# The decay factors of a state-space mixer's chunks: from matmul sums and exponentials to a VectorE scan over factors read back from memory

## The chip, the core and the metric

The kernel runs on one core of a Trainium2 chip, as one program of five engines: TensorE (PE in the profile, its weight loads PEld), VectorE (DVE), ScalarE (ACT), GpSimd (POOL) and SyncE (SP), which here does nothing but issue the DMAs. Each engine takes its instructions in the order in which they are written, and they meet at semaphores. The metric is the device time of one execution, in microseconds.

## The reference

A layer of four parts works on x, 64 sequences of 32 positions with 512 channels: a mixing of the channels by a condition vector, a selective state-space mixer (the attention-like part), a small grouped convolution with a context term, and a feed-forward part with a cluster test. The change is in the second part. What matters of it:

```python
proj = jnp.einsum('bld,pd->blp', hidden_states, in_proj_w)
xBC = jax.nn.silu(conv)                      # causal, 4 taps, over 6144 channels of proj
dt_p = jax.nn.softplus(dt + dt_bias)         # 64 heads
A = -jnp.exp(A_log)
dA = jnp.exp(dt_p * A)
dtx = dt_p[..., None] * x
def step(state, inp):
    dA_t, dtx_t, B_t, C_t = inp
    state = state * dA_t[..., None, None] + dtx_t[..., None] * B_t[:, :, None, :]
    y_t = jnp.einsum('bhpn,bhn->bhp', state, C_t)
    return (state, y_t)
y = ys + x * D                               # then a group norm, silu(gate) and out_proj
```

Since a sequence has only 32 positions, the kernel doesn't run the recurrence. Written out, y at position t is the sum over s up to t of (C_t . B_s) times dA_(s+1) ... dA_t times dt_s x_s. So for each head it needs a 32x32 table of decays, the product of the factors dA after s up to t.

## The kernel before, in words

**Tiling.** The 2048 rows (64 sequences x 32 positions) are 16 tiles of 128 rows, in 4 blocks of 4 tiles. The mixer runs in 32 stages: stage n handles one group of 8 heads (g, of 8) for one block (four tiles, 512 rows); `who(n)` gives half, group and block. Two consecutive stages use the same weights, so weights are loaded and split for pairs: the even stage comes first, and the next pair's input weights are split into a high and a low part during the odd stage (`split_w_hi` on ACT, `split_w_lo` on POOL), the output weights during the even one (`split_o_hi` on ACT, `split_o_lo` on DVE). All products are done as three matmuls of high and low parts.

**Slots.** A stage has ten slots m = 0 to 9. On every engine a function `stage(n)` walks through the slots, and what an engine does in a slot is written there by hand; that is what sets the order. PE's slot is `proj(n, m)`: 12 matmuls of 512 columns into one of three PSUM banks. The first six go through ACT (`evac`), three convolution taps on DVE (`taps`) and a SiLU on ACT; slots 6 to 9 are the gate. PE may start `proj` m+3 only when the bank of m is free. Between the projections PE does, for the stage before, `Y(n-1, 2)` and `Y(n-1, 3)` in slot 2 and the output products `O(n-1, i)`, 12 matmuls each, after slots 1, 3, 4 and 5; for this stage the products C.B (`G_all`, slot 2), the turning of x (`turn_x`, slots 7 and 9) and `Y(n, 0)`, `Y(n, 1)` at the end of slot 9. O(n-1, i) needs y in a high part (`y_high`, ACT) and a low one (`y_low`, POOL).

**The decays.** The logs of the factors, dt times A, are made once for each block as a [64 heads x 2, 256] tile `da`, with the softplus done on DVE as a series of 12 steps (`dt_series`, two-input operations of 256 columns, one reciprocal). PE turns step sizes and logs in slot 6 of stages 0, 1, 16 and 17 (`dt_turn`, the stages in `TURNED`). Then in each of the 32 stages: POOL multiplies the logs, as high and low part, with a mask of s up to t (`decays`, two operations of 128x1024, slot 6); PE sums them with a triangular matrix `uf` in `decay_sums`, four matmuls of 512 columns after slot 8; ACT takes the exponential (`expo`, two operations of 512 columns and an activation table load, slot 8); and DVE multiplies the decay table `Lt` with the masked C.B products (`decayed`, slot 9 for tiles 0 and 1, slot 1 of the next stage for 2 and 3). The result, in `big`, is what `Y` multiplies with the scaled x (`dtx`).

**Blocks.** Stages 0, 15 and 16 (`BLOCK_AT`) prepare the next block beside their own work: `mix_tile` in slots 2 to 5 and `dt_product`, 12 matmuls after slot 8. The softplus series of that block ran in slot 9 (two steps) and slots 4 and 5 of the next stage.

**DMA queue.** SP issues everything in one order: for a pair u, the four output weight tiles (`load_o`, the last waits for the split in slot 7 of the even stage), then ten input weight tiles for the next pair (`load_w`, three buffers, so each waits for the split of the third one before).

## Time and profile before

| | |
|---|---|
| median of 3 runs | 1578.07 us (1577.88 to 1579.59) |
| the profiled execution | 1578.78 us, of which the span is 1576.8 us |
| mean granted TensorE clock | 0.997 |
| busy share of the span | PE 98%, PEld 80%, DVE 67%, ACT 54%, POOL 50% |
| moved by DMA | 80.5 MB, 51 GB/s on average |

The span runs from the first to the last instruction, 2.0 us less than the execution's own time. The busy time of PE is the union of its matmuls; since they are pipelined, each row of a matmul is longer than the distance to the next start. Stage 0 begins at 20 us, stage 1 at 74 us, stage 10 ends at 521 us, stage 17 begins at 804 us, and the last one ends near 1475 us. Where a group of rows has an arrow after its numbers, that is the idle time of the engine just before these instructions, and what ended it.

### The profile page before, as it was taken

The page shows a single profiled execution, that of the slowest core. Times are in us where ns is not written, and L with a number is a line of the kernel's source. Part 1 is how long each engine was busy: PE and PEld are TensorE (multiplying, and loading weights), DVE is VectorE, ACT ScalarE, POOL GpSimd, SP SyncE. Part 2 cuts the span into 40 slices and gives each one's busy share as a digit, 9 for nine tenths or more (in the row PEclk, how much of TensorE's full clock was granted, in tenths as well). Part 3 has the DMA queues.
Part 4 walks back from the last instruction along what each step waited for, and adds up shares of the span by engine and source line. Part 5 has one row for each costly group of instructions (what it writes and reads, how often), then busy time and mean ns, then how long its engine had stood idle before and what let it go on. Part 6 is the DMA issues. An engine that isn't in the chain of part 4 may idle for free. (4 is left out here: it accounts for less than half of the span.)

```text
span 1576.8 us, 32373 instructions
## 1 busy us (share of the span) xinstructions
PE 1551.4 (98%) x12991; PEld 1268.9 (80%) x12991; DVE 1049.9 (67%) x1689; ACT 850.4 (54%) x1420; POOL 783.4 (50%) x747
## 2 busy tenths in 40 slices
PE   8999999999999999999999999999999999999997
PEld 6778888888888888888877888888888888888686
DVE  5877766665666756576877656667665656666566
ACT  4654556555555555555464555556555554545542
POOL 3565554546364554545354463644545463643506
PEclk9999999999999999999999999999999999999999
DMA  5110201111120201111012111102011111103212
GB/s 201 54 49 20 63 27 55 41 41 55 35 61 8 61 28 55 41 41 54 1 55 95 41 54 35 55 10 66 28 55 41 41 54 35 43 20 91 86 42 107
DMA packets 49524, 80.54 MB, mean 51 GB/s; under 512 B 4896, under 2 KB 13600, under 8 KB 49376
## 3 DMA queue, kind: packets, MB, share of 16 engines
q1 hardware_dynamic: 49376, 78.48, 15.9%
q8 instruction: 104, 1.70, 0.4%
q14 instruction: 44, 0.36, 0.1%
HBM read 70.07 MB, written 8.39 MB: 50 GB/s over the span
## 5 line engine op out<-in xcount | busy, mean ns | idle before, releaser
L434 PE MATMUL PS<-xh,wh 128*128 128x512 f32 x1280 | 519.9, 406 | 0.6 <-DVE xl L954 0.6
L434 PE MATMUL PS<-xh,wl 128*128 128x512 f32 x1280 | 500.8, 391 | 0.0
L434 PE MATMUL PS<-xl,wh 128*128 128x512 f32 x1280 | 499.1, 390 | 0.0
L1023 DVE SCALAR_TENSOR_TENSOR cb<-PS,P,cb 128x496 f32<-128x496 f32 (+2 forms) x576 | 412.6, 716 | 126.4 <-ACT cb L755 112.8
L1318 POOL TENSOR_TENSOR wl<-rw,wh 128x512 fp32r<-128x512 f32 x160 | 207.9, 1305 | 185.7 <-ACT wh L706 185.6
L1338 POOL TENSOR_TENSOR ysum<-yq 128x256 f32<-128x256 f32 x128 | 109.5, 856 | 356.2 <-ACT yq L802 356.1
L434 PEld LDWEIGHTS PS<-xh,wl 128*128 128x128 f32 x1280 | 240.5, 188 | 53.0
L434 PEld LDWEIGHTS PS<-xh,wh 128*128 128x128 f32 x1280 | 240.9, 188 | 50.3 <-issue 1.0
L434 PEld LDWEIGHTS PS<-xl,wh 128*128 128x128 f32 x1280 | 241.4, 189 | 44.6
L755 ACT ACTIVATE cb<-PS,P 128x512 f32<-128x512 f32 x192 | 148.5, 773 | 198.1 <-PE PS L434 198.1
L547 PE MATMUL PS<-oh,yh 128*128 128x512 f32 x512 | 200.1, 391 | 1.3 <-POOL yl L1347 0.8
L547 PE MATMUL PS<-oh,yl 128*128 128x512 f32 x512 | 199.9, 391 | 0.0
L547 PE MATMUL PS<-ol,yh 128*128 128x512 f32 x512 | 199.2, 389 | 0.0
L802 ACT ACTIVATE yq<-y 128x512 f32<-128x512 f32 x128 | 81.1, 633 | 202.0 <-DVE y L1067 190.3
L1053 DVE TENSOR_TENSOR big<-Lt,gmt 128x512 f32<-128x512 f32 x128 | 102.6, 843 | 117.0 <-ACT Lt L794 117.0
L762 ACT ACTIVATE big<-PS 128x512 f32<-128x512 f32 x128 | 76.3, 596 | 147.6 <-PE PS L434 147.2
L777 ACT ACTIVATE big<-cb 128x512 f32<-128x512 f32 x192 | 119.7, 623 | 65.6 <-DVE cb L1023 65.6
L1092 DVE SCALAR_TENSOR_TENSOR acc<-PS,rs,acc 128x512 f32<-128x512 f32 x128 | 93.1, 749 | 89.1 <-issue 47.3
L1355 POOL TENSOR_TENSOR rs<-vr,mh 128x1 f32<-128x1 f32 (+1 forms) x95 | 57.1, 601 | 160.1 <-DVE vr L1082 160.1
L1043 DVE TENSOR_TENSOR dtx<-PS,dtt 128x512 f32<-128x512 f32 x128 | 82.1, 683 | 60.0 <-PE PS L477 59.7
L547 PEld LDWEIGHTS PS<-oh,yh 128*128 128x128 f32 x512 | 96.1, 188 | 21.9 <-ACT yh L809 2.2
L547 PEld LDWEIGHTS PS<-oh,yl 128*128 128x128 f32 x512 | 96.1, 188 | 20.1
(195 smaller groups left out, 2142.6 us busy)
## 6 DMA issues: line engine op xcount, KB each, us to landing
rw<-in_w_in SPq DMA_DIRECT2D x160, 256.0 KB, 2.7
ro<-in_w_out SPq DMA_DIRECT2D x64, 256.0 KB, 2.9
x2s<-acc SPq DMA_DIRECT2D x16, 256.0 KB, 3.0
out_x<-acc SPq DMA_DIRECT2D x16, 256.0 KB, 2.6
acc<-in_x SPq DMA_DIRECT2D x3, 1024.0 KB, 9.3
wh<-x2s SPq DMA_DIRECT2D x8, 256.0 KB, 3.8
wl<-x2s SPq DMA_DIRECT2D x8, 256.0 KB, 4.5
acc<-in_x SPq DMA_DIRECT2D x4, 256.0 KB, 4.6
```

What stands on the lines that cost most here:

```text
L434: mm = e.matmul(PS[:, proj_bank(n, m), :], w[:, m, 128 * k:128 * k + 128], v[:, k, a:a + 512], start=(i == 0), stop=(i == 11))
L547: mm = e.matmul(PS[:, O_bank(n, i), :], v[:, r, 128 * j:128 * j + 128], w[:, j, :], start=(q == 0), stop=(q == 11))
L755: e.activation(cb[:, z % 2, :], PS[:, proj_bank(n, m), :], ACT.Identity, bias=P[:, P_CB + c:P_CB + c + 1], scale=P[:, P_CW + 4 * c + 3:P_C ...
L762: e.activation(gate[:, m - 6, :], PS[:, proj_bank(n, m), :], ACT.Silu).then_inc(evac_ok.sem, 1)
L777: e.activation(dst, cb[:, (6 * n + m) % 2, :], ACT.Silu).then_inc(silu_ok.sem, 1)
L802: e.activation(yq[:, :], y[:, i % 2, :], ACT.Square).then_inc(yq_ok.sem, 1)
L1023: e.scalar_tensor_tensor(out=cv[:, :, d:32], in0=pv[:, :, 0:32 - d], scalar=P[:, P_CW + 4 * c + 3 - d:P_CW + 4 * c + 4 - d], in1=cv[:, :, ...
L1043: e.tensor_tensor(dtx[:, r, :].rearrange("p (j v c) -> p j v c", j=4, v=2), PS[:, b0:b0 + 2, 256 * r:256 * r + 256].rearrange("p v (j c) - ...
L1053: e.tensor_tensor(Mb[:, i % 2], bc(Lt[:, 256 * i:256 * i + 256].rearrange("p (h o t) -> p h o t", h=8, o=1), 128, 8, 2, 32), bc(gmt[:, i, ...
L1092: e.scalar_tensor_tensor(out=acc[:, T, :], in0=PS[:, O_bank(n, i), :], scalar=rs[:, i:i + 1], in1=acc[:, T, :], op0=ALU.mult, op1=ALU.add) ...
L1318: e.tensor_tensor(wl[:, m, :], rw[:, q % RW, :], f(wh[:, m, :]), ALU.subtract).then_inc(w_lo.sem, 1)
L1338: e.tensor_tensor(ysum[:, :], yq[:, 0:256], yq[:, 256:512], ALU.add).then_inc(ys1.sem, 1)
```

## The change

The 32x32 table of a head obeys a recurrence along t: L[s, t] = L[s, t-1] times dA_t, and L[s, s] = 1. The change makes the table by that recurrence, with one VectorE instruction for each stage (`tensor_tensor_scan`, multiply, then maximum): its first input `dab` holds the factors, the same row for all 32 partitions s of a sequence, with 0 for the first position of each row of 32, which resets the scan; its second, `diag`, is 1 where t = s and 0 elsewhere. The name `Lt` is kept; its columns are now ordered head, tile, position.

- The factors are made once for each block: in slot 4 of the stages in `TURNED`, ACT takes the exponential of `da` (`rates_exp`), POOL sets the first positions to 0 (`first_rates`), and SP stores them to a DRAM tensor `rates` in two DMAs of 64 partitions, in pieces of 256 bytes.
- In each stage SP reads back four pieces, each one 4 KB row of DRAM read for 32 partitions (`load_rate`, 4 x 128 KB); this waits until the scan of the stage before has read the buffer. DVE runs the scan in slot 7.
- `decay_sums`, `expo` and the POOL `decays` go, and so do two of the four turns in `dt_turn` and what split the turned logs.
- `decayed` for tiles 0 and 1 moves from slot 9 to 8.
- The series of a block has its steps in slots 1, 2 and 3 of stage 0, four each, and otherwise in slot 9 and slots 2 and 3 of the next stage. `dt_product` moves from after slot 8 to slot 7 (for blocks 1 to 3 into another PSUM bank), `dt_first` on ACT from slot 9 to 8.

The core of the diff:

```diff
+        dab = sb("dab", [128, 1024])
+        diag = sb("diag", [128, 1024])
...
+        rate_t = dt_x
...
+        def D_bank(b):
+            return PY[0] if b else PT
...
+            def store_rate(b):
+                sp.wait_ge(rate_zero, b)
+                for r in range(2):
+                    dst = bass.AP(rates.tensor, b * 32768 + 64 * r, [[128, 64], [8192, 4], [1, 64]])
+                    src = rate_t[64 * r:64 * r + 64, :].rearrange("p (q a) -> p q a", q=4)
+                    e.dma_start(dst, src).then_inc(rate_out[b].sem, 16)
+
+            def load_rate(n):
+                half, g, tb = who(n)
+                b = 2 * half + tb
+                sp.wait_ge(rate_out[b], 1)
+                if n >= 1:
+                    sp.wait_ge(L_ok, n - 1)
+                for q in range(4):
+                    src = bass.AP(rates.tensor, b * 32768 + 8192 * q + 1024 * g, [[0, 32], [1, 1024]])
+                    e.dma_start(dab[32 * q:32 * q + 32, :], src).then_inc(ld_rate.sem, 16)
+
...
                 for j in range(4):
+                    if u % 8 == 0 and j == 2:
+                        store_rate(u // 4)
+                        load_rate(2 * u)
                     load_o(u, j)
+                if u % 8:
+                    load_rate(2 * u + 1)
                 if u < 15:
                     for m in range(10):
                         load_w(u + 1, m)
+                        if u % 8 == 0 and m == 7:
+                            store_rate(u // 4 + 1)
+                        if u % 8 == 0 and m == 8:
+                            load_rate(2 * u + 1)
+                if u % 8 != 7:
+                    load_rate(2 * u + 2)
                 if u == 8:
                     for T in range(8):
...
+                if b >= 2:
+                    pe.wait_ge(acc_ok, ({2: 14, 3: 15}[b], 3))
                 i = 0
                 for k in range(4):
                     for w, v in ((wdh, xh), (wdh, xl), (wdl, xh)):
-                        mm = e.matmul(PS[0:64, PT, :], w[:, 64 * k:64 * k + 64], v[:, k, a:a + 512], start=(i == 0), stop=(i == 11))
+                        mm = e.matmul(PS[0:64, D_bank(b), :], w[:, 64 * k:64 * k + 64], v[:, k, a:a + 512], start=(i == 0), stop=(i == 11))
...
-                pe.wait_ge(d_done, b)
+                pe.wait_ge(d_step, (b, 10))
...
-                for i, src in enumerate((dr[:, 0:128], dr[:, 128:256], da[:, 0:128], da[:, 128:256])):
-                    mm = e.transpose(PS[:, SEG[0], 128 * i:128 * i + 128], src, ident)
+                for i in range(2):
+                    mm = e.transpose(PS[:, SEG[0], 128 * i:128 * i + 128], dr[:, 128 * i:128 * i + 128], ident)
                 mm.then_inc(DT_ok.sem, 1)
...
-            def decay_sums(n):
...
-                for r in range(2):
-                    if r == 0 and n - 1 in BLOCK_AT:
-                        pe.wait_ge(a_hi, BLOCK_AT[n - 1])
-                        pe.wait_ge(a_lo, BLOCK_AT[n - 1])
-                    if n >= 1:
-                        pe.wait_ge(acc_ok, (n - 1, 1 + 2 * r))
-                    else:
-                        pe.wait_ge(x_lo, 5 + 2 * r)
-                    e.matmul(PS[:, SEG[r], :], uf[:, :], avh[:, 512 * r:512 * r + 512], start=True, stop=False)
-                    e.matmul(PS[:, SEG[r], :], uf[:, :], avl[:, 512 * r:512 * r + 512], start=False, stop=True).then_inc(seg_ok.sem, 1)
...
-                    pe.wait_ge(L_ok, (n, 0))
-                    if n in BLOCK_AT:
-                        pe.wait_ge(d_max, (BLOCK_AT[n], 1))
+                    if n in TURNED:
+                        pe.wait_ge(dt_ok, TURNED[n])
...
-                    pe.wait_ge(L_ok, (n, 1))
                     pe.wait_ge(dtx_ok, (n, 1))
+                    if n in BLOCK_AT:
+                        pe.wait_ge(d_max, (BLOCK_AT[n], 1))
...
-                    if m == 8:
-                        decay_sums(n)
                         if b is not None:
                             dt_product(b)
...
                     act.wait_ge(DT_ok, b - 1)
+                    act.wait_ge(rate_out[b - 1], 1)
...
+            def rates_exp(b):
+                act.wait_ge(d_done, b)
+                e.activation(rate_t.rearrange("p (q i t) -> p q i t", q=4, i=2),
+                             da[:, :].rearrange("p (i q t) -> p q i t", i=2, q=4), ACT.Exp).then_inc(rate_exp.sem, 1)
+
             def dt_turned(b):
                 a = 4 * (b % 2)
-                dt, av = (PS[:, SEG[0], k:k + 256].rearrange("p (i r c) -> p i r c", i=2, r=2) for k in (0, 256))
                 act.wait_ge(DT_ok, b)
-                e.copy(dtt[:, a:a + 4, :].rearrange("p (r i) c -> p i r c", r=2), dt).then_inc(dt_ok.sem, 1)
-                e.copy(ah[:, a:a + 4, :].rearrange("p (r i) c -> p i r c", r=2), av).then_inc(a_hi.sem, 1)
+                e.copy(dtt[:, a:a + 4, :].rearrange("p (r i) c -> p i r c", r=2),
+                       PS[:, SEG[0], 0:256].rearrange("p (i r c) -> p i r c", i=2, r=2)).then_inc(dt_ok.sem, 1)
...
-            def expo(n):
-                for r in range(2):
-                    act.wait_ge(seg_ok, (n, r))
-                    if n >= 1:
-                        act.wait_ge(M_ok, (n - 1, 3))
-                    e.activation(Lt[:, 512 * r:512 * r + 512], PS[:, SEG[r], :], ACT.Exp).then_inc(L_ok.sem, 1)
...
-                act.wait_ge(seg_ok, (n, 1))
...
-                    if b is not None and m == 9:
+                    if b is not None and m == 8:
...
+                    if n in TURNED and m == 4:
+                        rates_exp(TURNED[n])
...
-                    if m == 8:
-                        expo(n)
...
-            def dt_turned(b):
...
+            def decays(n):
+                dve.wait_ge(ld_rate, n)
+                if n == 0:
+                    dve.wait_ge(diag_ok)
+                e.tensor_tensor_scan(Lt[:, :], dab[:, :], diag[:, :], 0.0, ALU.mult, ALU.max).then_inc(L_ok.sem, 1)
...
-                dve.wait_ge(L_ok, (n, i // 2))
+                dve.wait_ge(L_ok, n)
                 dve.wait_ge(G_masked, n)
-                e.tensor_tensor(Mb[:, i % 2], bc(Lt[:, 256 * i:256 * i + 256].rearrange("p (h o t) -> p h o t", h=8, o=1), 128, 8, 2, 32),
+                e.tensor_tensor(Mb[:, i % 2], bc(Lt[:, :].rearrange("p (h i t) -> p h i t", h=8, i=4)[:, :, i:i + 1, :], 128, 8, 2, 32),
...
-                series = {0: (0, {1: (0, 2), 2: (2, 4), 3: (4, 7), 4: (7, 9), 5: (9, 12)})}.get(n)
...
+                        e.tensor_copy(diag[:, :].rearrange("p (a t) -> p a t", a=32),
+                                      bc(C[:, C_EQ:C_EQ + 32].rearrange("p (a t) -> p a t", a=1), 128, 32, 32)).then_inc(diag_ok.sem, 1)
+                    if m == 7:
+                        decays(n)
                     if m == 8:
                         scale_turned(n, 0)
                         scale_turned(n, 1)
-                    if m == 9:
                         decayed(n, 0)
                         decayed(n, 1)
-                    if n == 0 and 1 <= m <= 5:
-                        dt_series(0, *((0, 2), (2, 4), (4, 7), (7, 9), (9, 12))[m - 1])
+                    if n == 0 and 1 <= m <= 3:
+                        dt_series(0, 4 * m - 4, 4 * m)
                     if b is not None and m == 9:
-                        dt_series(b, 0, 2)
-                    if n - 1 in BLOCK_AT and m in (4, 5):
-                        dt_series(BLOCK_AT[n - 1], *((2, 7), (7, 12))[m - 4])
-                    if m == 6 and n in TURNED:
-                        dt_turned(TURNED[n])
+                        dt_series(b, 0, 4)
+                    if n - 1 in BLOCK_AT and m in (2, 3):
+                        dt_series(BLOCK_AT[n - 1], *((4, 8), (8, 12))[m - 2])
...
-            def decays(n):
-                half, g, tb = who(n)
-                b = 2 * half + tb
-                pool.wait_ge(dt_ok, b)
-                pool.wait_ge(a_hi, b)
-                pool.wait_ge(a_lo, b)
-                if n >= 1:
-                    pool.wait_ge(O_ok, (n - 1, 3))
-                for src, dst, done in ((ah, avh, av_hi), (al, avl, av_lo)):
-                    e.tensor_tensor(dst.rearrange("p (i h t) -> p i h t", i=4, h=8),
-                                    bc(f(src[:, 4 * tb:4 * tb + 4, 8 * g:8 * g + 8]).rearrange("p i (h o) -> p i h o", o=1), 128, 4, 8, 32),
-                                    bc(C[:, C_V:C_V + 32].rearrange("p (a b t) -> p a b t", a=1, b=1), 128, 4, 8, 32),
-                                    ALU.mult).then_inc(done.sem, 1)
+            def first_rates(b):
+                pool.wait_ge(rate_exp, b)
+                e.memset(rate_t.rearrange("p (a t) -> p a t", t=32)[:, :, 0], 0.0).then_inc(rate_zero.sem, 1)
...
-                    if m == 6:
-                        decays(n)
+                    if m == 4 and n in TURNED:
+                        first_rates(TURNED[n])
...
-    cst[:, C_V:C_V + 32] = s[:, None] <= np.arange(32)[None, :]
+    cst[:, C_EQ:C_EQ + 32] = s[:, None] == np.arange(32)[None, :]
```

TensorE at the border of slots 8 and 9 of an even stage. L434 (L461 in the changed kernel) is a matmul of `proj`, with xh, xl, wh and wl the high and low parts of activations and weights; L453 and L454 are those of `decay_sums`. Before:

```order
L434 MATMUL PS<-xl,wh 128x512
L434 MATMUL PS<-xh,wl 128x512
L453 MATMUL PS<-yh,uf 128x512 [waits s_avl,s_avh]
L454 MATMUL PS<-yl,uf 128x512
L453 MATMUL PS<-yh,uf 128x512 [waits s_acc]
L454 MATMUL PS<-yl,uf 128x512
L434 MATMUL PS<-xh,wh 128x512 [waits s_ev,s_w_lo,s_w_hi]
```

With the change:

```order
L461 MATMUL PS<-xh,wh 128x512
L461 MATMUL PS<-xl,wh 128x512
L461 MATMUL PS<-xh,wl 128x512
L461 MATMUL PS<-xh,wh 128x512 [waits s_ev,s_w_lo,s_w_hi]
L461 MATMUL PS<-xl,wh 128x512
```

The four matmuls and their two waits are gone, and the projection of slot 9 follows that of slot 8.

VectorE from slot 6 to slot 9 of an even stage: acc is the accumulated output, ol the low part of the output weights, dtx the scaled and turned x, big<-Lt,gmt the product of decays and masked C.B. Before:

```order
L1092 SCALAR_TENSOR_TENSOR acc<-PS,rs,acc 128x512 [waits s_acc,s_rs,s_O]
L1011 SCALAR_TENSOR_TENSOR ol<-ro,P,oh 128x512 [waits s_o_hi] x2
L1043 TENSOR_TENSOR dtx<-PS,dtt 128x512 [waits s_T]
L1043 TENSOR_TENSOR dtx<-PS,dtt 128x512
L1011 SCALAR_TENSOR_TENSOR ol<-ro,P,oh 128x512 [waits s_o_hi]
L1053 TENSOR_TENSOR big<-Lt,gmt 128x512 [waits s_Gm,s_L]
L1053 TENSOR_TENSOR big<-Lt,gmt 128x512
L1011 SCALAR_TENSOR_TENSOR ol<-ro,P,oh 128x512 [waits s_o_hi]
```

With the change:

```order
L1096 SCALAR_TENSOR_TENSOR acc<-PS,rs,acc 128x512 [waits s_acc,s_rs,s_O]
L1015 SCALAR_TENSOR_TENSOR ol<-ro,P,oh 128x512 [waits s_o_hi]
L1010 SCALAR_TENSOR_TENSOR Lt<-dab,diag 128x1024 [waits s_ld_rate]
L1015 SCALAR_TENSOR_TENSOR ol<-ro,P,oh 128x512 [waits s_o_hi]
L1047 TENSOR_TENSOR dtx<-PS,dtt 128x512 [waits s_T]
L1047 TENSOR_TENSOR dtx<-PS,dtt 128x512
L1057 TENSOR_TENSOR big<-Lt,gmt 128x512 [waits s_Gm,s_L]
L1057 TENSOR_TENSOR big<-Lt,gmt 128x512
L1015 SCALAR_TENSOR_TENSOR ol<-ro,P,oh 128x512 [waits s_o_hi] x2
```

The scan (L1010) stands between the first two splits, behind a wait for the factors, and the decay products come ahead of the last two splits.

VectorE in slots 2 and 3 of stage 1, from the accumulation of slot 2 on; cb is a convolution tap, gmt the masked C.B, y and yg the output before and after the gate. Before:

```order
L1092 SCALAR_TENSOR_TENSOR acc<-PS,rs,acc 128x512 [waits s_rs,s_O]
L1023 SCALAR_TENSOR_TENSOR cb<-PS,P,cb 128x16x31 [waits s_ev]
L1023 SCALAR_TENSOR_TENSOR cb<-PS,P,cb 128x16x30 [waits s_tap]
L1023 SCALAR_TENSOR_TENSOR cb<-PS,P,cb 128x16x29 [waits s_tap]
L1031 TENSOR_TENSOR gmt<-PS,C 128x256 [waits s_M,s_G]
L1067 TENSOR_TENSOR y<-PS,big 128x512 [waits s_yg,s_yq,s_Y]
```

With the change:

```order
L1096 SCALAR_TENSOR_TENSOR acc<-PS,rs,acc 128x512 [waits s_rs,s_O]
L992 TENSOR_SCALAR dr<-pb 128x256 [waits s_dch]
L994 SCALAR_TENSOR_TENSOR dr<-dr,pb 128x256 [waits s_dch] x3
L1027 SCALAR_TENSOR_TENSOR cb<-PS,P,cb 128x16x31 [waits s_ev]
L1027 SCALAR_TENSOR_TENSOR cb<-PS,P,cb 128x16x30 [waits s_tap]
L1027 SCALAR_TENSOR_TENSOR cb<-PS,P,cb 128x16x29 [waits s_tap]
L1035 TENSOR_TENSOR gmt<-PS,C 128x256 [waits s_M,s_G]
L1071 TENSOR_TENSOR y<-PS,big 128x512 [waits s_yg,s_yq,s_Y]
```

Four steps of the series stand now ahead of the taps of slot 2 and of y for tile 2.

## Rows read from the trace of the kernel before

**Rows 1.** The page, busy microseconds, share of the span and instructions of each engine.
```profile
PE 1551.4 (98%) x12991; PEld 1268.9 (80%) x12991; DVE 1049.9 (67%) x1689; ACT 850.4 (54%) x1420; POOL 783.4 (50%) x747
```

**Rows 2.** Two stretches: length, busy PE, PEld, DVE, ACT, POOL, clock, DMA.
```profile
120.00:800.00 680.00, 680.00 (x5630) 557.17 (x5620) 456.26 (x698) 373.17 (x596) 342.24 (x326) 1.00 0.13 41
854.00:1400.00 546.00, 546.00 (x4606) 447.48 (x4605) 355.83 (x544) 299.65 (x475) 281.67 (x270) 1.00 0.14 43
```

**Rows 3.** PE's waits: line waited, releaser, microseconds in total, times, longest.
```profile
PE PS L453 <- issue: 4.5, 3, 2.1
PE PS L489 <- ACT big L777: 3.7, 1, 3.7
PE PS L414 <- DVE da L997: 1.0, 3, 0.4
```

**Rows 4.** PE's groups of instructions: shape, count, busy microseconds, mean ns.
```profile
L453 PE MATMUL PS<-yh,uf 128*128 128x512 f32 x64 | 25.2, 393 | 4.5 <-issue 4.5
L454 PE MATMUL PS<-yl,uf 128*128 128x512 f32 x64 | 24.9, 389 | 0.0
...
L414 PE MATMUL PS<-C,da 128*128 128x128 f32 x8 | 1.5, 273 | 0.0
```

**Rows 5.** Timeline of PE, end of stage 10: start, length, instruction.
```profile
515.88 0.39 PE L453 MATMUL PS<-yh,uf 128*128 128x512 f32 x1
...
516.78 0.39 PE L434 MATMUL PS<-xh,wh 128*128 128x512 f32 x1
...
520.24 0.46 PE L509 MATMUL PS<-big,dtx 64*64 64x64 f32 x16
```

**Rows 6.** Timeline of PE, slots 8 and 9 of stage 0.
```profile
64.58 0.40 PE L403 MATMUL PS<-xh,wdh 128*64 128x512 f32 x1
...
68.93 0.39 PE L434 MATMUL PS<-xh,wh 128*128 128x512 f32 x1
```

**Rows 7.** A stretch of stage 0, with the columns of rows 2.
```profile
66.00:68.00 2.00, 2.00 (x6) 1.10 (x5) 0.40 (x1) 0.78 (x2) 0.00 (x0) 0.50 0.15 58
```

**Rows 8.** Timeline of DVE, slots 6 to 9 of stage 10.
```profile
508.55 1.67 DVE L1011 SCALAR_TENSOR_TENSOR ol<-ro,P,oh 128x512 fp32r<-128x512 f32 x1
512.74 0.75 DVE L1011 SCALAR_TENSOR_TENSOR ol<-ro,P,oh 128x512 fp32r<-128x512 f32 x1 [2.52 <-ACT oh L713]
513.40 1.28 DVE L1043 TENSOR_TENSOR dtx<-PS,dtt 128x512 f32<-128x512 f32 x2
...
518.62 1.29 DVE L1053 TENSOR_TENSOR big<-Lt,gmt 128x512 f32<-128x512 f32 x2 [3.27 <-ACT Lt L794]
```

**Rows 9.** DVE's groups of instructions, with the columns of rows 4.
```profile
L1067 DVE TENSOR_TENSOR y<-PS,big 128x512 f32<-128x512 f32 x128 | 87.5, 684 | 31.3 <-PE PS L509 31.3
...
L981 DVE RECIPROCAL dr<-da 128x256 f32<-128x256 f32 x4 | 7.0, 1752 | 0.1
...
L993 DVE SCALAR_TENSOR_TENSOR dr<-pb,da 128x256 f32<-128x256 f32 x4 | 1.7, 423 | 0.1
```

**Rows 10.** Timeline of DVE in stage 1, the series where it stood.
```profile
97.81 1.26 DVE L987 TENSOR_SCALAR dr<-pb 128x256 f32<-128x256 f32 x1
99.11 0.88 DVE L989 SCALAR_TENSOR_TENSOR dr<-dr,pb 128x256 f32<-128x256 f32 x2
```

**Rows 11.** Timeline of POOL in stage 1: the low part of y, tile 2.
```profile
92.26 1.30 POOL L1347 TENSOR_TENSOR yl<-yg,yh 128x512 fp32r<-128x512 f32 x1
```

**Rows 12.** Timeline of PE in stage 1: the first matmul of O(0, 2).
```profile
94.64 0.39 PE L547 MATMUL PS<-oh,yh 128*128 128x512 f32 x1
```

**Rows 13.** The page, DMA issues: count, KB each, median microseconds from issue to landing.
```profile
rw<-in_w_in SPq DMA_DIRECT2D x160, 256.0 KB, 2.7
...
acc<-in_x SPq DMA_DIRECT2D x3, 1024.0 KB, 9.3
```

**Rows 14.** Timeline of SP, stage 10: the ten input weight loads.
```profile
513.94 44.93 SPq L299 DMA_DIRECT2D rw<-in_w_in  x10
```

**Rows 15.** Timeline of ACT, stage 11, slot 0: the first of these weights is split.
```profile
525.06 0.61 ACT L706 CAST wh<-rw 128x512 fp32r<-128x512 f32 x1
```

48 lines of the change are left out of this document (14 added, 34 removed).

## The prediction

> **What bounds the kernel now.** First the busy shares: TensorE is busy 98% of the span, VectorE 67%, the other two about half [rows 1]. A share near 100% could still hide a loop through another engine that ends just in time, so the next view is the busy time by stretch: from 120 to 800 us PE is busy 680.00 of 680.00 us, from 854 to 1400 us all 546, at full clock, while DVE has 456 and 356 [rows 2]. In nearly all of the 32 stages PE never waits. What it takes out of those stages comes off the time, as long as nobody else's work becomes late. Third, the list of PE's waits: 4.5 us in three places ahead of the decay sums (L453), 3.7 us once ahead of the C.B products in stage 0 (L489), 1.0 us in three places ahead of the turns (L414) [rows 3]. The first and the last of these lie on the chain softplus series, turns, split, POOL mask, decay sums, in the stages where a block's decays are first made.
>
> **What a matmul costs.** A row of the decay sums has a mean of 389 to 393 ns [rows 4], but these lengths overlap. The cost is the distance between starts: the first of the four starts at 515.88, the projection behind them at 516.78 [rows 5], so four cost 0.90 us, 0.225 each.
>
> **The sum, part by part.** It starts from the profiled execution, 1578.78 us.
>
> 1. The decay sums go from 32 stages: 32 x 0.90 = 28.8 us, all on PE's path.
> 2. Their waits go: 4.5 us, and with them the reason, since the sums' operands no longer exist. The waits ahead of the turns, 1.0 us, go as well: the series now ends in slot 3 and the turns stay in slot 6, and they wait no longer for the last step.
> 3. Eight of 16 turns go. Their busy time is 1.5 us [rows 4]; with the same overlap as above (0.225 of 0.39) that is 0.9 us.
> 4. Behind the longest of the waits, 2.1 us in stage 0, the clock fell: the granted clock is 0.50 (1.2 instead of 2.4 GHz) from 66 to 68 us [rows 7], and the 12 matmuls of `dt_product` take from 64.58 to 68.93, 4.35 us [rows 6], where 12 x 0.225 = 2.7 us would do. 1.65 us come back if PE doesn't pause there.
> Together 36.85 us.
>
> **What replaces it, and what covers it.**
>
> 5. The scan. No row shows one. From below: two-input operations take 684 ns for 512 columns and 423 ns for 256 [rows 9], 1.02 ns a column and 0.16 us fixed, so 1024 columns at that rate are 1.2 us. From above: the one row in which a column takes several passes is the reciprocal, 1752 ns for 256 columns [rows 9], 7.0 us for 1024. I take 2.3 us, twice the rate of an ordinary operation, since a multiply and a maximum that feed each other are much closer to an ordinary row than to a division. What it may take, from the timeline of an even stage [rows 8]: DVE is free after the first split at 508.55 + 1.67 = 510.22. Behind the scan are the second split 0.75, two scalings 1.28 and two decay products 1.29, together 3.32. PE wants the products for Y at 520.24 [rows 5], less the 0.90 removed: 519.34. So the scan has 519.34 - 510.22 - 3.32 = 5.8 us; at 2.3 it costs nothing. Today's products end at 518.62 + 1.29 = 519.91, 0.3 us ahead of Y: the change turns a tight chain (sums, table load, exponential, product) into one with 3.5 us to spare. Odd stages have no split there and more room. The covers are DVE's idle times of 2.52 and 3.27 us in slots 7 to 9 [rows 8]; without them 32 x 2.3 = 74 us would be at stake.
>
> The Trainium skill's page "DVE: opcode table, instruction layouts, handler registers and perf-mode slots" (section Datapath and trigger behaviour) says of the built-in scan that it "runs at half throughput". By that rule, the estimate is 2.3 us, the sum stays, and the rival of a slow scan would fall away; no run so far shows it.
>
> 6. The factor loads: 4 x 128 KB for a stage. DVE's scan waits for them, and behind it on DVE are the split, the scalings and the products, for which PE waits. They are issued when the scan before has ended, so they have a whole stage, some 44 us; even at the 9.3 us of the 1024 KB loads [rows 13] they cost DVE nothing. In the four stages where they come behind the stores of the new factors the lead is only two to three slots of some 4.5 us, against two landings in a row of 3 to 5 us each; I take nothing and leave this to the range. What is queued behind them on SP is the rival below.
>
> 7. ACT loses two exponentials and a table load a stage, POOL two operations of 1024 columns. Neither is on the path, nothing is earned.
>
> 8. The series moves earlier, and this is what costs. In stages 1 and 17 four steps now stand in slot 2, ahead of y for tile 2. A step of 256 columns beside a POOL operation took 1.26 us, later ones 0.44 each (0.88 for two) [rows 10]; so 1.26 + 3 x 0.43 = 2.55 us of delay for y. From y the way leads over ACT and POOL: the low part ends at 92.26 + 1.30 = 93.56 [rows 11], and O(0, 2) starts at 94.64 [rows 12], 1.1 us of slack. PE will wait some 1.4 us in each, 2.8 in all. Bounds: nothing if DVE catches up; with all four steps at 1.26, 5.0 - 1.1 = 3.9 each. Stage 16 has mixing tiles on PE in slots 2 and 3 and so more room; nothing is taken.
>
> 9. In stage 0 two more steps, 2 x 0.42 [rows 9], come ahead of the taps of slot 1, on which the C.B products wait already 3.7 us [rows 3]: 0.85 us. The four steps of slots 2 and 3 stand ahead of taps that PE needs three slots later.
>
> The sum: 1578.78 - 36.85 + 2.8 + 0.85 = 1545.6 us for a run like the profiled one; the median of the runs is 0.7 lower, which gives **1545 us**, 2.1% less.
>
> **The rivals.**
>
> *Block stages cost more.* Terms 8 and 9 at their upper ends (3.9 each in stages 1 and 17, 2.5 in stage 0), a like wait in stage 16, and behind two of these pauses a fallen clock at 1.65 us each as in term 4: about 10 us more than in my sum, 1555. For it: the waits on DVE's series are shown to be tight, and ACT has to wait inside slot 4 for the end of the series before it goes on. Against: before the change, DVE carried the same steps one or two slots later without any wait of PE but the turns'. I give this 1551 to 1558, centre 1554.
>
> *The scan is slow.* At 7.0 us it passes the 5.8 us by 1.2 in 16 even stages: 1545 + 19 = 1564. Only the reciprocal row speaks for it.
>
> *The factor loads hold up the weights (the slower side).* After slot 7 of an even stage SP issues the next pair's first weights at 513.94 [rows 14]; now they come behind the factor loads. ACT splits them at 525.06 [rows 15], 11.1 us later, and a load lands in 2.7 [rows 13]: 8.4 us to spare, and 1.1 us of slack in front of the output products. If the four loads keep the queue L us, PE loses L - 9.5 in each of 15 odd stages. The point from which the kernel is slower than before is 33/15 = 2.2 beyond, L = 11.7 us. One after another at the landing time of the 256 KB loads they take 4 x 2.7 = 10.8, a loss of 20 us (1565); at 12.5 us the time is 1590. Against it: 1024 KB landed in 9.3 us [rows 13], so 512 KB, if they overlap, in 4.7. Each load reads one 4 KB row 32 times and writes 32 partitions, for which no row stands.
>
> The Trainium skill's page "SBUF — State Buffer" (section "Can I just issue two DMAs to hit both halves?") speaks against the change here: transfers to different halves of the partitions don't add up but serialize, and a transfer to 32 partitions gets 189 GB/s. By that, 512 KB are an estimated 2.8 us of transfer, far from the point; the sum would stay. No run so far shows it.
>
> *PE's pitch is not PE's.* If some loop of another engine set the stage's pitch and PE only looked full, the time would stay at 1577. Against: the 680 us without one gap.
>
> **How the numbers follow.** Chances: my forecast (1540 to 1551) 0.78; block stages 0.10; slow scan 0.03; loads holding up the weights 0.04, half of it beyond the time before; pitch kept 0.02; below 1540, more given back in the start than I see, 0.03. Without any new wait the sum is 1541.3, and the shape of the gain allows 1 us less: low end 1540. The high end takes in the bounds of terms 8 and 9: 1555. That leaves out about 0.14. A measurement of this kernel can tell some 0.2%, 3 us, from no change. Faster by more: 0.95; within: 0.02 (pitch kept); slower by more: 0.03.
>
> **What the profile of the changed kernel would show.** PE: 128 matmuls less, no wait between slots 8 and 9; in the stretch of the long middle still busy without gaps; the stage's pitch 0.90 us shorter. PE's list of waits: none at the turns, new ones of 1 to 2 us ahead of the output products in stages 1 and 17, 4.5 us at the C.B products of stage 0, and the clock at 1.00 from 60 to 72 us. DVE: a scan of about 2.3 us in slot 7, never waiting for its factors but perhaps in stages 0, 1, 16 and 17; the decay products more than 3 us ahead of Y. The factor loads landing in 3 to 6 us, the first weight split of odd stages not waiting for a DMA. I am wrong if the scan exceeds 5.8 us, if the loads exceed 9.5, or if PE shows short waits in every stage.

## The result and the profile after

The changed kernel takes **1551.64 us** in the median of 4 runs (1551.49 to 1553.26), the kernel before 1578.06 beside it; the ratio is 0.9833, 95% interval [0.9816, 0.985]. That is 26.4 us less, where the prediction had 33. It lies inside the range (1540 to 1555), near the rival "block stages cost more" (1551 to 1558). The profiled execution took 1551.53 us, its span 1549.7.

Busy shares of the page, then the two stretches of [rows 2] with the same columns:
```profile
PE 1522.1 (98%) x12855; PEld 1244.9 (80%) x12855; DVE 1109.2 (72%) x1717; ACT 753.7 (49%) x1306; POOL 657.8 (42%) x687
```
```profile
120.00:800.00 680.00, 677.05 (x5642) 553.64 (x5641) 492.12 (x725) 334.86 (x554) 284.00 (x300) 1.00 0.18 52
854.00:1400.00 546.00, 546.00 (x4529) 446.90 (x4528) 388.56 (x562) 262.79 (x438) 233.47 (x247) 1.00 0.19 55
```
PE has 136 instructions less than in [rows 1]: 128 sums and 8 turns. DVE, with the scan, rose from 67 to 72%, ACT and POOL fell. In the long middle 2.95 us of idle time have appeared that were not there before: the two mixing-tile waits below.

PE's list of waits, against [rows 3] (line waited, releaser, microseconds, times, longest; L498 is the C.B products, L557 the output products, L413 the first matmul of a mixing tile, L959 `mixed_lo`; where `issue` stands, the profile names no releaser):
```profile
PE PS L498 <- ACT big L790: 4.7, 1, 4.7
PE PS L557 <- issue: 3.3, 2, 1.6
PE PS L413 <- DVE xl L959: 3.0, 2, 2.3
```
The waits ahead of the sums and the turns are gone. Those ahead of C.B and of the output products came as forecast. The third line was in no term of the sum.

DVE's groups of the new work (mean ns before the idle time), and one of the series' lines, against the last of [rows 9]; then the factor loads on the page (count, KB, microseconds to landing):
```profile
L1010 DVE TENSOR_TENSOR_SCAN Lt<-dab,diag 128x1024 f32<-128x1024 f32 x32 | 74.0, 2313 | 5.5 <-DMA dab<-rates 5.5
...
L998 DVE SCALAR_TENSOR_TENSOR dr<-pb,da 128x256 f32<-128x256 f32 x4 | 5.5, 1385 | 0.1
```
```profile
dab<-rates SPq DMA_DIRECT2D x128, 128.0 KB, 3.1
```
The scan takes 2.3 us. The same series step that took 423 ns before takes 1385 now: nothing in it changed but its place, and that is the second thing the sum didn't have.

**Where the gain was made and lost.** From the first C.B product of a stage to that of the next, an ordinary stage took 44.54 us before and takes 43.69 now: 0.85 less, in 25 stretches alike. Between the C.B products of stages 0 and 1 the change gains 5.7 us (the wait, the turns, the clock). The first C.B product of all comes 1.2 us later than before. Between those of stages 16 and 17 it takes 55.13 us instead of 51.33 and loses 3.8. PE's waits there, and the clock behind the second, which is granted 0.50 for two microseconds (columns of [rows 2]):
```profile
751.49 0.47 PE L413 MATMUL PS<-ab,xb 128*128 128x512 f32 x1 [0.68 <-DVE xl L959]
760.60 0.47 PE L413 MATMUL PS<-ab,xb 128*128 128x512 f32 x1 [2.27 <-DVE xl L959]
```
```profile
760.00:762.00 2.00, 1.40 (x8) 1.39 (x9) 1.96 (x5) 1.97 (x3) 0.11 (x1) 0.82 0.00 0
762.00:764.00 2.00, 2.00 (x8) 1.61 (x7) 1.64 (x3) 1.27 (x3) 0.00 (x0) 0.50 0.31 66
764.00:766.00 2.00, 2.00 (x9) 1.64 (x8) 0.01 (x1) 0.00 (x0) 0.00 (x0) 0.83 0.51 135
```
DVE ahead of that wait, in slot 3 of stage 16, and POOL at the same time:
```profile
754.25 0.69 DVE L996 SCALAR_TENSOR_TENSOR pb<-dr,pb 128x256 f32<-128x256 f32 x1
754.97 1.41 DVE L998 SCALAR_TENSOR_TENSOR dr<-pb,da 128x256 f32<-128x256 f32 x1
756.48 0.78 DVE L1000 SCALAR_TENSOR_TENSOR dr<-dr,pb 128x256 f32<-128x256 f32 x1
757.29 0.43 DVE L1002 TENSOR_SCALAR da<-dr,scol 128x256 f32<-128x256 f32 x1
757.64 2.21 DVE L1027 SCALAR_TENSOR_TENSOR cb<-PS,P,cb 128x496 f32<-128x496 f32 x3
759.77 0.68 DVE L959 TENSOR_TENSOR xl<-PS,xh 128x512 fp32r<-128x512 f32 x1
```
```profile
754.61 1.48 POOL L1340 TENSOR_TENSOR yl<-yg,yh 128x512 fp32r<-128x512 f32 x1
756.05 0.92 POOL L1331 TENSOR_TENSOR ysum<-yq 128x256 f32<-128x256 f32 x1
```
Four steps that should take 1.7 us hold up the taps by 3.4, from 754.25 to 757.64. `mixed_lo` follows the taps, and the mixing tile of slot 4 starts 0.15 us after `mixed_lo` ends.

### The profile page after: what moved, and what is told of

It is laid out like the page before. It is cut to its first block and busy times, and to the rows that moved or that the text cites. A ratio compares the mean times of both kernels' runs of the same rounds, so it can differ in the third digit from the quotient of the medians.

```text
span 1549.7 us, 31996 instructions
## 1 busy us (share of the span) xinstructions
PE 1522.1 (98%) x12855; PEld 1244.9 (80%) x12855; DVE 1109.2 (72%) x1717; ACT 753.7 (49%) x1306; POOL 657.8 (42%) x687
## 3 DMA queue, kind: packets, MB, share of 16 engines
q8 instruction: 102, 1.67, 0.4%
## 5 line engine op out<-in xcount | busy, mean ns | idle before, releaser
L461 PE MATMUL PS<-xh,wh 128*128 128x512 f32 x1280 | 518.7, 405 | 0.6 <-DVE xl L959 0.6
L461 PE MATMUL PS<-xh,wl 128*128 128x512 f32 x1280 | 501.1, 391 | 0.0
L461 PE MATMUL PS<-xl,wh 128*128 128x512 f32 x1280 | 500.4, 391 | 0.0
L461 PEld LDWEIGHTS PS<-xh,wl 128*128 128x128 f32 x1280 | 240.5, 188 | 52.5
L461 PEld LDWEIGHTS PS<-xh,wh 128*128 128x128 f32 x1280 | 240.9, 188 | 51.3 <-issue 1.0
L461 PEld LDWEIGHTS PS<-xl,wh 128*128 128x128 f32 x1280 | 241.1, 188 | 45.3
L557 PE MATMUL PS<-oh,yh 128*128 128x512 f32 x512 | 200.7, 392 | 4.9 <-issue 3.3
L557 PE MATMUL PS<-oh,yl 128*128 128x512 f32 x512 | 200.3, 391 | 0.0
L557 PE MATMUL PS<-ol,yh 128*128 128x512 f32 x512 | 199.8, 390 | 0.0
L1071 DVE TENSOR_TENSOR y<-PS,big 128x512 f32<-128x512 f32 x128 | 87.6, 685 | 83.8 <-PE PS L519 83.8
L557 PEld LDWEIGHTS PS<-oh,yh 128*128 128x128 f32 x512 | 96.6, 189 | 26.4 <-issue 4.1
L1057 DVE TENSOR_TENSOR big<-Lt,gmt 128x512 f32<-128x512 f32 x128 | 116.4, 950 | 0.0
L557 PEld LDWEIGHTS PS<-oh,yl 128*128 128x128 f32 x512 | 96.4, 188 | 20.2
```

Of the source, the lines that this page charges most:

```text
L461: mm = e.matmul(PS[:, proj_bank(n, m), :], w[:, m, 128 * k:128 * k + 128], v[:, k, a:a + 512], start=(i == 0), stop=(i == 11))
L557: mm = e.matmul(PS[:, O_bank(n, i), :], v[:, r, 128 * j:128 * j + 128], w[:, j, :], start=(q == 0), stop=(q == 11))
L1057: e.tensor_tensor(Mb[:, i % 2], bc(Lt[:, :].rearrange("p (h i t) -> p h i t", h=8, i=4)[:, :, i:i + 1, :], 128, 8, 2, 32), bc(gmt[:, i, :] ...
L1071: e.tensor_tensor(y[:, r, :].rearrange("p (j q t) -> p j q t", j=4, q=2), PS[:, PY[0]:PY[0] + 2, 256 * r:256 * r + 256].rearrange("p q (j ...
```

## Experiments

The kernels below are the changed kernel with one edit or, where the text says so, several; only the last starts from the kernel before. "Pitch" is the distance from the first C.B product of one stage to that of the next, as above, and "from C.B 16 to C.B 17" is that distance for stage 16. The times are medians. The kernel before was run again beside each group of experiments and took 1577.9 to 1578.8 us, so a difference of less than 1 us between two experiments says nothing by itself; the stretches of the traces have to tell. Each trace is one execution of its kernel. In the code, lines left out are marked by three dots.

**1. Stage 16: the series behind `mixed_lo`.**
```
-                    if n - 1 in BLOCK_AT and m in (2, 3):
+                    if n in (1, 17) and m in (2, 3):
                         dt_series(BLOCK_AT[n - 1], *((4, 8), (8, 12))[m - 2])
...
                     if b is not None and 2 <= m <= 5:
                         mixed_lo(4 * b + m - 2)
+                    if n == 16 and m in (2, 3):
+                        dt_series(BLOCK_AT[n - 1], *((4, 8), (8, 12))[m - 2])
```


> The changed kernel with one edit: in stage 16 alone the four series steps of slot 2 and the four of slot 3 stand behind the taps and behind mixed_lo on VectorE instead of ahead of them. Theory (the series delays mixed_lo, and the mixing tiles of slots 3 and 4 wait for it): TensorE's two waits ahead of the mixing tiles in stage 16 (0.68 and 2.27 us) go, and with them the fallen clock from 762 to 764 us, some 1.65 us more. Together 4.6 us less than the changed kernel: 1547.0 us. Rival (the two waits come from something else that the change moved, such as dt_product in slot 7, the scan, or SP's queue): the waits stay where they are and the time stays at 1551.6.

1548.76 us (ratio 0.9809 [0.9795, 0.9824]), 2.9 less. The stretch from C.B 16 to C.B 17 takes 51.09 us instead of 55.13: **4.0 us** come back there. PE's wait and the clock around it:
```profile
PE PS L413 <- DVE xl L959: 0.7, 1, 0.7
```
```profile
762.00:764.00 2.00, 2.00 (x13) 1.71 (x12) 1.63 (x3) 1.99 (x3) 0.00 (x0) 1.00 0.26 55
```
The wait of 2.27 us and the fallen clock are gone, one of 0.7 stays. The theory holds for its place. In the total 1.1 us is missing because stage 0, whose instructions are the same, took longer: behind the wait ahead of C.B, which is 4.7 us in both, the clock came back later here. The changed kernel has 0.50 at 38 to 40 us and 0.73 at 40 to 42; this one has:
```profile
38.00:40.00 2.00, 2.00 (x36) 1.65 (x37) 1.90 (x5) 1.51 (x3) 0.90 (x1) 0.50 0.00 0
40.00:42.00 2.00, 2.00 (x6) 1.58 (x5) 1.97 (x4) 0.00 (x0) 2.00 (x2) 0.50 0.20 70
42.00:44.00 2.00, 2.00 (x7) 1.56 (x6) 1.97 (x3) 0.13 (x1) 1.92 (x2) 0.62 0.89 311
```
Behind a pause of one and the same length the two traces thus differ by 1.1 us. Why, isn't shown; all four executions of this kernel lie within 0.4 us of each other, which speaks against the chance of a single one.

**2. Stages 1 and 17: all eight steps in slot 3, behind the taps.**
```
-                    if n - 1 in BLOCK_AT and m in (2, 3):
+                    if n == 16 and m in (2, 3):
                         dt_series(BLOCK_AT[n - 1], *((4, 8), (8, 12))[m - 2])
...
+                    if n in (1, 17) and m == 3:
+                        dt_series(BLOCK_AT[n - 1], 4, 12)
```


> The changed kernel with one edit: in stages 1 and 17 all eight series steps stand in slot 3 behind the taps, none in slot 2. Theory (the steps of slot 2 delay y of tile 2, and O(0, 2) and O(16, 2) wait for its low part): the two waits of 1.63 and 1.64 us ahead of the output products go, 3.3 us less than the changed kernel: 1548.4 us. The series ends some 2.5 us later, so VectorE's waits for the factors grow from 1.9 to 4.4 us in stage 1 and from 2.7 to 5.2 in stage 17, which the room of odd stages (7.5 us, without a split) still hides. Rival (the later factors are what counts): TensorE waits instead ahead of Y in stages 1 and 17, up to 3 us each, and the time is 1551 to 1555.

1556.23 us, 4.6 more: 3.1 of it from C.B 1 to C.B 2 and from C.B 17 to C.B 18, most of the rest in stage 0, where the clock came back later as in experiment 1. The two output-product waits are gone, but the rival's are there:
```profile
PE PS L519 <- DVE big L1057: 3.9, 4, 1.0
```
The factors arrive later, and what stands behind them has less room than assumed. DVE in stage 1 (the changed kernel had the scan at 106.50 and the two products in 2.39 us):
```profile
109.07 2.73 DVE L1010 TENSOR_TENSOR_SCAN Lt<-dab,diag 128x1024 f32<-128x1024 f32 x1 [1.64 <-DMA dab<-rates]
111.73 1.25 DVE L1047 TENSOR_TENSOR dtx<-PS,dtt 128x512 f32<-128x512 f32 x2
112.91 3.44 DVE L1057 TENSOR_TENSOR big<-Lt,gmt 128x512 f32<-128x512 f32 x2
```
The products end at 116.35, while some 1.3 us is what two of them take with POOL idle ([rows 8]). In stages 1 and 17 the series is on the path twice: too early it delays y, too late it delays the factors.

**3. Stage 0: the series behind the taps.**
```
-                    if n == 0 and 1 <= m <= 3:
-                        dt_series(0, 4 * m - 4, 4 * m)
...
                     if m < 6:
                         taps(n, m)
+                    if n == 0 and 1 <= m <= 3:
+                        dt_series(0, 4 * m - 4, 4 * m)
```


> The changed kernel with one edit: in stage 0 the series steps of slots 1, 2 and 3 stand behind the taps of their slot instead of ahead. Theory: the first four steps take 3.0 us ahead of the taps of slot 1 (0.42 + 1.75 + 0.42 + 0.42), so the wait of 4.7 us ahead of the C.B products falls to 1.7, and if the shorter pause doesn't let the clock fall, 1.65 us come back as well: 3.0 to 4.6 us less, 1547.0 to 1548.6 us. Rival (the C.B products wait for something that is not VectorE's, such as the splits on ScalarE): the wait stays at 4.7 or falls by less than 1, and the time stays at 1551 to 1552.

1557.25 us, 5.6 more. The wait ahead of C.B fell to 1.8 us, as expected. But a new one stands two slots later, at 55.61:
```profile
PE PS L413 <- DVE ab L950: 7.2, 1, 7.2
```
Moved by 2.9 us, the steps ran beside POOL's mixing weights. DVE, and POOL at that time:
```profile
37.12 1.46 DVE L988 TENSOR_TENSOR da<-pb,dr 128x256 f32<-128x256 f32 x1
38.61 2.49 DVE L990 TENSOR_TENSOR pb<-da 128x256 f32<-128x256 f32 x1
...
42.51 2.21 DVE L1027 SCALAR_TENSOR_TENSOR cb<-PS,P,cb 128x496 f32<-128x496 f32 x3
...
45.02 4.65 DVE L994 SCALAR_TENSOR_TENSOR dr<-dr,pb 128x256 f32<-128x256 f32 x3
```
```profile
38.25 2.57 POOL L1311 TENSOR_TENSOR big<-big 128x1024 f32<-128x1024 f32 x1
```
In the changed kernel L988 and L990 took 0.42 us each and L994 1.34 for three. The step at 38.61 ends at 41.10, 0.3 us after POOL's operation at 38.25 ends (40.82): it waits for the whole of it. The taps, which read PSUM, take 2.21 us for three with POOL busy or idle. The Trainium skill's page "SBUF — State Buffer" (section SBUF: two separate sides) gives the rule: VectorE with two SBUF inputs and a GpSimd operation that reads SBUF share a port pair under an exclusive lock that is held for the whole instruction. This trace agrees: 2.49 us for the step with two SBUF inputs, no change for the taps.

**4. The edits of experiments 1 to 3 together.** 

> The changed kernel with the three edits together: stage 16 behind mixed_lo, stages 1 and 17 in slot 3 behind the taps, stage 0 behind the taps. Theory: the gains add, 4.6 + 3.3 + 3.0 to 4.6, together 10.9 to 12.5 us less than the changed kernel: 1539.2 to 1540.8 us, and no wait of TensorE over 1 us before the last stage but the one ahead of the C.B products of stage 0. Rival: pauses that go in one place come back in the next, and the sum is less than half of it, over 1546.

1556.22 us: stage 16's gain is there, with the losses of experiments 2 and 3 (a wait of 7.7 us ahead of a mixing tile in stage 0). Neither the theory's number nor its reason held. The rival's did: pauses move on.

**5. Stages 1 and 17: the four steps of slot 2 at its head** (with experiment 1; the steps of slot 3 stay where they were).
```
+                    if n in (1, 17) and m == 2:
+                        dt_series(BLOCK_AT[n - 1], 4, 8)
                     if n:
                         if m in (2, 5, 6):
                             variance(n - 1, {2: (0,), 5: (1, 2), 6: (3,)}[m])
```


> The changed kernel with the edit of stage 16 (series behind mixed_lo) and one more: in stages 1 and 17 the four series steps of slot 2 stand at the head of the slot, ahead of the variance and the output addition, where VectorE waited 1.23 us for POOL's reciprocal root. Theory (what delays y of tile 2 is the time that VectorE spends on the steps after that wait): 1.2 us of the 2.7 that the steps take are hidden, so the two waits of 1.63 us ahead of the output products fall to 0.4 each; 2.4 us less than the kernel with stage 16 alone: 1546.3 us. Rival (the steps at the head run beside POOL and take 1.2 us each, or they delay the output addition so that TensorE waits elsewhere): no gain or a loss, 1548.5 to 1551.

1547.27 us (0.9803 [0.979, 0.9817]), 1.5 less than experiment 1 by the medians and 1.0 by the spans of the traces, 1.0 short of the theory. Both output-product waits are gone, but the variance was delayed, and the C.B products need it:
```profile
PE PS L498 <- DVE vr L1086: 2.4, 2, 1.2
```

**6. The fastest one run.** Experiment 1, the four steps of stages 1 and 17 between the variance and the output addition, and in stage 0 the taps of slot 1 ahead of everything else in the slot.
```
                             variance(n - 1, {2: (0,), 5: (1, 2), 6: (3,)}[m])
+                        if n in (1, 17) and m == 2:
+                            dt_series(BLOCK_AT[n - 1], 4, 8)
...
+                    if n == 0 and m == 1:
+                        taps(n, m)
                         mix_operands(4)
                         mix_operands(5)
```


> The changed kernel with stage 16 behind mixed_lo and two more edits. In stages 1 and 17 the four series steps of slot 2 stand between the variance and the output addition, so that the variance is not delayed and the wait for POOL's root still hides them: the two waits of 1.2 us that the kernel with the steps at the head of the slot had ahead of the C.B products go, 2.4 us. In stage 0 the taps of slot 1 stand first, ahead of the operands for mixing tiles 4 and 5 and of the series; VectorE idled there for 3.06 us until POOL had the mixing weights. The taps then end near 31.6 us instead of 37.2, and the steps keep their distance from POOL's next work: the wait of 4.7 us ahead of the C.B products goes, and with it the fallen clock behind it, about 1.2 us. Together 8.3 us less than 1547.3: 1539 us. Rival (moving the taps only shifts the wait to mixing tile 4, whose operands come later, as in the kernel with the series behind the taps): a wait of several us ahead of a mixing tile in stage 0, and 1544 to 1548 us.

**1545.98 us** (0.9797 [0.9783, 0.9812]), less than both kernels and 1.3 us less than experiment 5, whose interval overlaps with it: that it is faster than experiment 5 isn't shown. The theory had 1539. In stages 1 and 17 no wait is left, as expected. In stage 0 the wait ahead of C.B is gone as well, but:
```profile
PE PS L461 <- DVE cb L1027: 5.1, 1, 5.1
PE PS L413 <- DVE bd L947: 3.0, 3, 1.7
```
The steps again ran into POOL's mixing weights, three of them in 5.28 us:
```profile
39.32 5.28 DVE L994 SCALAR_TENSOR_TENSOR dr<-dr,pb 128x256 f32<-128x256 f32 x3
```
ScalarE's split of a weight had come earlier with the rest, and POOL's work follows it: the edit moved both sides of the collision. From 34 to 48 us DVE is busy 13.8 of 14 us, what it waits for POOL inside an instruction counted in. The edit of stage 0 gained nothing: C.B 1 starts at 83.87 us here and at 84.13 in experiment 5, of which 1.2 us is the wait that the other edit removed. So by the traces it cost some 0.9 us, and the kernel without it, which was not run, may be the fastest.

**7. Four matmuls put back** in slot 8, on operands that have long been there; nobody reads their result.
```
+                for k in range(4):
+                    e.matmul(PS[:, SEG[0], :], wdh[:, 0:128], xh[:, k, a:a + 512], start=(k % 2 == 0), stop=(k % 2 == 1))
...
+                    if m == 8:
+                        four_more(n)
```


> The changed kernel with four matmuls of 512 columns put back in slot 8 of all 32 stages, on operands that have long been there, with a result that nobody reads: the reverse of the removed decay sums, without their wait. Theory (TensorE's own work sets the pitch, 0.855 us for four): 32 x 0.855 = 27.4 us more than the changed kernel: 1579.0 us, pitch of a stage 44.54 us. By the 0.90 of the prediction it would be 28.8 us more: 1580.4. Rival (the removed matmuls were partly hidden or some other loop set the pitch): the pitch stays below 44.3 and the time below 1572.

1581.70 us (1.0021 [1.0012, 1.003]), 30.1 more. The pitch is 44.59 us, 0.905 more than 43.69, in every ordinary stage; PE shows the distance directly:
```profile
514.38 1.07 PE L471 MATMUL PS<-xh,wdh 128*128 128x512 f32 x4
515.29 0.39 PE L461 MATMUL PS<-xh,wh 128*128 128x512 f32 x1
```
32 x 0.905 = 29.0; most of the rest is stage 0, where PE's clock again came back later, 1.4 us by the trace. So four matmuls cost 0.905, as the prediction had it, and my later 0.855 was wrong as their price. The change loses 0.05 us a stage elsewhere: by the distances of starts, the two projections ahead of the first turn of x take 5.66 us instead of 5.62, and the one ahead of Y of tiles 2 and 3 takes 2.94 instead of 2.90, with the matmuls back too; one other projection gains 0.03. Why, stays open.

**8. The scan three and four times over** (three more instead of two in the second kernel).
```
+                for k in range(2):
+                    e.tensor_tensor_scan(Lt[:, :], dab[:, :], diag[:, :], 0.0, ALU.mult, ALU.max).then_inc(L_one.sem, 1)
+                    dve.wait_ge(L_one, (n, k))
```


> The changed kernel with the scan of each stage done three times over, one behind the other, 6.85 us instead of 2.28. By the trace of the changed kernel the products end 3.4 us ahead of Y in stage 10, and VectorE idles 1.3 us between scan and products, so 4.7 us more are free in even stages, some 4.9 in odd ones: 4.57 us more should cost nothing, 1551.6 us. By the prediction's room of 5.8 us for the scan it would cost 1.1 us in each of 16 even stages: 1569 us. Rival (VectorE's longer scan also holds up POOL's weight splits, which ran slower beside it, and TensorE waits for those): waits ahead of projections, over 1560 us.

> The changed kernel with the scan done four times over, 9.13 us. 6.85 us more than in the changed kernel against 4.7 us of room in even stages and 4.9 in odd ones: 2.1 us of wait ahead of Y in each of 32 stages, some 65 us: 1617 us. By the prediction's room of 5.8 us it would be 3.3 us in 16 even stages and 1.6 in odd ones: 1631 us. Rival (a pause in every stage lets the clock fall each time, 1.65 us more each): over 1660 us.

Three: 1570.26 us, where I had 1551.6. The pitches of ordinary even stages stay at 43.69, those of odd ones are 43.76 to 43.81, so 4.6 us more of scan cost nothing in an even stage and at most 0.12 in an odd one: there the room is as expected. The spans differ by 17.5 us, and nearly all of it arose elsewhere: 8.4 us at the end of stage 1 and 6.4 at that of stage 17, where the scan waits for its factors and PE up to 3.5 us for the scaled x, 2.8 at that of stage 0 (of it 1.8 a wait ahead of an output product for the low part of y), 1.4 less in stage 16. The sum by the prediction's room, 1569, was met by its number, but not by its reason. Four: 1668.16 us in the one execution that there is, above every expectation but the last. Stage 10 costs 1.7 us, stage 11 5.9; the ordinary odd stages cost 3.3 to 6.0. PE in stage 11, its turns first, then the stretch behind them with the columns of [rows 2]:
```profile
597.35 0.71 PE L486 MATMUL PS<-C,big 64*128 64x64 f32 x16 [2.06 <-DVE dtx L1050]
599.00 1.99 PE L519 MATMUL PS<-big,dtx 64*64 64x64 f32 x64 [0.94 <-DVE big L1060]
```
```profile
600.00:602.00 2.00, 2.00 (x43) 1.69 (x36) 0.91 (x2) 0.22 (x1) 0.00 (x0) 0.50 0.41 155
```
Two things I had not counted: the second turn of x waits for `dtx` and comes before Y, so the room ends there; and in odd stages a scan beside POOL's splits takes 3.20 us instead of 2.28 and POOL's two splits 4.76 instead of 2.6, the same lock. In stage 11 the clock fell behind the pause, in stage 10 it stayed at 1.00, so the last rival's fall in every stage isn't there either.

**9. The factors loaded twice and three times,** SP standing still in between (`range(2)` in the second kernel).
```
+                for k in range(1):
+                    for q in range(4):
...
+                        e.dma_start(dab[32 * q:32 * q + 32, :], src).then_inc(ld_pre.sem, 16)
+                    sp.wait_ge(ld_pre, (n, k))
```


> The changed kernel with the factors of each stage loaded twice, the second time when the first has landed; SP stands still until then, some 4.9 us more a stage (1.8 to issue, 3.1 to land). The trace of the changed kernel has the first weights of the next pair issued at 504.21 and split at 511.7, 7.5 us later, and a load lands in 2.8: 4.7 us to spare. So no or next to no wait in the even stages, and 1551.6 to 1555 us; in stages 1 and 17, where the factors are awaited already, up to 3 us each for the scan on top. The prediction's rule, L less 9.5 with L now 2.7 + 4.9 = 7.6, gives no loss at all for the weights. Rival (each load already holds up the weights through the queues): over 1570 us.

> The changed kernel with the factors of each stage loaded three times, one after the other, SP standing still some 9.8 us more a stage. With 4.7 us to spare it is 5.1 us too late for the weights of each of 15 pairs, less about 1 us of slack on TensorE: 15 x 4.1 = 62 us, 1613 us, and TensorE's waits stand ahead of the projections of even stages or ahead of the output products. The prediction's rule, L less 9.5 with L = 12.5, gives 15 x 3.0 = 45 us: 1597 us. Rival (the weights have a stage more of room than this, since three tiles of raw weights lie ahead): under 1565 us.

Twice: 1561.55 us, 9.9 more, where I had up to 3.4 and up to 3 on top in each of stages 1 and 17. All ordinary stages keep 43.69 us. The spans of the traces differ by 11.0 us, which lie in the ends of stages 1 (4.6), 17 (3.0) and 0 (2.8, about half of it the clock) and ahead of C.B 0 (0.6). DVE waits for factors 19.1 us in 3 places, up to 8.0, instead of 5.5. Stage 1 loses more than the 3 us that I allowed, and stage 0 I hadn't counted. Three times: 1591.87 us, below both numbers that I had (1613 and, by the prediction's rule, 1597). ACT waits for weights, from 500 to 700 us, in the changed kernel not at all, with two loads 1.3 us, with three
```profile
ACT wh L720 <- DMA rw<-in_w_in: 9.9, 2, 5.1
```
which is 9.8 - 4.7 = 5.1 as worked out. But PE waits only 14.0 us for it, in 11 waits ahead of the C.B products, 1.7 at most from 500 to 700 us; some 3.4 of ACT's 5.1 us are hidden, not the some 1 us that I took. By the pitches the ordinary stages lose 18.3 us, and the block stages the rest. So, by an estimate from these rows, ACT begins to wait when the queue is kept about 7.4 us (2.7 + 4.7) and PE at about 10.8 (7.4 + 3.4). The prediction's 9.5 lies between, and the change keeps the queue 2.7 us in stage 10 and 1.7 to 3.2 in all stages.

**10. The kernel before with the early series alone.**
```
-                    if n == 0 and 1 <= m <= 5:
-                        dt_series(0, *((0, 2), (2, 4), (4, 7), (7, 9), (9, 12))[m - 1])
+                    if n == 0 and 1 <= m <= 3:
+                        dt_series(0, 4 * m - 4, 4 * m)
                     if b is not None and m == 9:
-                        dt_series(b, 0, 2)
-                    if n - 1 in BLOCK_AT and m in (4, 5):
-                        dt_series(BLOCK_AT[n - 1], *((2, 7), (7, 12))[m - 4])
+                        dt_series(b, 0, 4)
+                    if n - 1 in BLOCK_AT and m in (2, 3):
+                        dt_series(BLOCK_AT[n - 1], *((4, 8), (8, 12))[m - 2])
```


> The kernel before with one part of the change alone: the softplus series in slots 9, 2 and 3 (1, 2 and 3 in stage 0) instead of 9, 4 and 5 (1 to 5). Theory: the waits ahead of the decay sums (4.5 us) and the turns (1.0) go or shrink below 1, with the fallen clock behind the longest (1.65); in exchange 1.0 us more ahead of the C.B products of stage 0, 3.3 us in two waits ahead of the output products of stages 1 and 17, and 4.6 us in stage 16 (two waits ahead of mixing tiles and the clock behind them). Sum 1.8 us more than before: 1579.8 us. Rival (the waits of stage 16 need another part of the change, such as dt_product in slot 7 or the scan): no wait ahead of mixing tiles in stage 16, and 1575 us.

1585.61 us (1.0044 [1.0029, 1.0059]), 7.6 **more** than the kernel before; the profiled execution is the shortest of the four, 1583.44, and its span is 4.6 more. The waits of stage 16 need nothing but the early series:
```profile
PE PS L384 <- DVE xl L954: 3.3, 2, 2.3
```
From C.B 16 to C.B 17 it takes 55.72 us, against 51.33. Between C.B 0 and C.B 1 it gains 3.4 us, ahead of C.B 0 it loses 1.2. The output products wait 5.5 us in 5 places, not 3.3 in two. The runs differ by 3 us among themselves, so of the total the sign is sure, not the last two microseconds.

## Why the prediction was right, and where it was 6 us off

**Terms 1 to 3, exact in their mechanism.** Four matmuls cost 0.905 (experiment 7). Net of the 0.05 that the change loses elsewhere the term is 27.4 instead of 28.8: -1.4 us. The waits at sums and turns are gone. The turns have no measurement of their own. That the pitch fell by nearly the whole price in all ordinary stages settles the rival "PE's pitch is not PE's".

**Term 4, right.** The clock is 1.00 from 60 to 72 us. The row that answers to [rows 7]:
```profile
66.00:68.00 2.00, 2.00 (x30) 1.46 (x32) 1.97 (x2) 1.99 (x4) 0.00 (x0) 1.00 0.23 88
```

**Term 5, right in size.** 2.28 us for the scan, 2.3 taken; in stage 10 the products end 3.4 us ahead of Y. The Trainium skill's rule ("DVE: opcode table, instruction layouts, handler registers and perf-mode slots", Datapath and trigger behaviour) of half throughput agrees with it: 2.28 us against the 1.2 that 1024 columns take at the rate of an ordinary operation. The room of 5.8 us was too small for even stages, in which 6.9 us of scan cost nothing. One reason is in [rows 8]: the first split was taken at the 1.67 us that it needed beside POOL's `decays`, which the change removes. After the change, in stage 10:
```profile
496.06 0.74 DVE L1015 SCALAR_TENSOR_TENSOR ol<-ro,P,oh 128x512 fp32r<-128x512 f32 x1
496.72 2.28 DVE L1010 TENSOR_TENSOR_SCAN Lt<-dab,diag 128x1024 f32<-128x1024 f32 x1
```
That is 0.93 us more room than the sum had, and term 7's "nothing is earned" is right for PE's time but not for DVE's. For odd stages "more room" was wrong: POOL's splits take it away, and with four scans an odd stage costs about three times what an even one does (experiment 8).

**Term 6, right, with one gap.** The loads land in 3.1 us, the weights don't wait. From the first issue to the last landing the four take 3.9 to 6.8 us, 5.2 in the median; the 2.8 us that the prediction estimated from the page are transfer alone, which no row here separates. What keeps the queue is only the issuing, 1.7 to 3.2 us. But "two to three slots" of lead in block stages is no slack: DVE waits there 5.5 us, and most of what delays the factors further reaches PE (experiments 2, 8 and 9).

**Term 8, the step that failed.** For stages 1 and 17 it gave 1.4 us each and 1.6 was measured. For stage 16 it said "more room, nothing is taken". It looked at how much work PE has in those slots and not at what the mixing tiles wait for: `mixed_lo` stands behind the series on DVE. Cost: 3.0 us of waits and what the clock lost behind the second, together 4.65 us against an ordinary stage. Experiment 1 gave back 4.0 of it, and experiment 10 made it appear in the kernel before. In the same term a step was priced at 0.43 us, with 1.26 as its dearest. Beside POOL's y work it takes 0.7 to 1.4, beside POOL's mixing weights up to 2.5. The trace of before could have told: the two steps just ahead of those in [rows 10], beside a low part of y and a weight split on POOL, took more than this bound.
```profile
94.98 1.36 DVE L983 TENSOR_TENSOR da<-pb,dr 128x256 f32<-128x256 f32 x1
96.38 1.40 DVE L985 TENSOR_TENSOR pb<-da 128x256 f32<-128x256 f32 x1
```

**Term 9:** 4.7 us at C.B against 4.55 forecast; 0.15 over.

Together: 1.4 + 4.65 + 0.5 (term 8) + 0.15 = 6.7 us against a gap of 5.9 between the two profiled numbers (1545.6 and 1551.53). The difference of 0.8 us lies mostly in stage 0: from C.B 0 to C.B 1 the change gained 5.7 us, where terms 1 to 4 have 5.0 there; which instructions gave the rest isn't shown. The measured time lies just above the forecast's own 1540 to 1551, at the lower edge of the rival "block stages cost more"; it even named "a like wait in stage 16". Its own sum was too small, though: 5.0 and 1.65 at the upper ends, 1.4 to 3.9 for a like wait and 3.3 for the clock are 11.4 to 13.9 us more, not about 10. Its chance of 0.10 was too low, since the queue behind the series in stage 16 was to be seen in the code. The slow scan, the held-up weights and the kept pitch are each refuted.

**The early series is a bad trade by itself** (experiment 10: 7.6 us). That it pays as what lets the factors be ready in slot 7 is argued from experiment 2, in which later steps delayed the factors; the scan with the series in its old place was not run.

## What to carry to other kernels

Where a step moves on an engine, list everything queued behind it there until its new end and ask which of it another engine waits for; how busy that other engine is says nothing about it. The price of a small VectorE operation with both inputs in SBUF depends on what GpSimd does at its new time, so read its cost beside the neighbours that it will have. And a pause that is removed can come back one or two slots later, as in experiments 3, 4 and 6, if the engine that caused it has no time to spare there: look there before counting it.

## What the runs showed of the hardware

- A VectorE operation of 256 columns from SBUF, 0.42 us alone, took 1.4 to 2.5 us when a POOL operation had begun before it, and in experiment 3's row at 38.61 ended 0.3 us behind POOL's. POOL is held up by the scan in turn: in the changed kernel two weight splits begun at 107.09, during a scan, took 4.03 us instead of 2.6. The taps, with PSUM as one input, took 2.21 us for three in both cases.
- The scan is 2.28 us for 128 x 1024 fp32, 2.2 ns a column, and up to 3.2 us beside a POOL operation that began before it (experiment 8).
- After a pause of 4.7 us in one and the same place the clock was back at 1.00 from 42 us on in the traces of the changed kernel and of both kernels of experiment 8, and only from 43.5 us or later in six others (experiments 1, 2, 5, 7 and both of 9) whose instructions there are the same. Against the changed kernel this cost the six 1.1 to 1.4 us each. Nothing here shows what decides it, and two kernels that differ by a microsecond or two may differ in this alone.
